# Weaving a block's message rows in pairs of slots, with both norms of the node update on ScalarE and another order of the blocks

## What is computed

```python
def _genconv(h, edge_attr, src, dst, w1, b1, g1, bb1, w2, b2, t):
    msg = relu(h[src] + edge_attr) + EPS_MSG
    m = msg * t
    seg_max = segment_max(m, dst)
    ex = exp(m - seg_max[dst])
    denom = segment_sum(ex, dst)
    alpha = ex / (denom[dst] + 1e-16)
    agg = segment_sum(msg * alpha, dst)
    out = h + agg
    z = relu(_layernorm(out @ w1 + b1, g1, bb1))      # 128 wide
    return z @ w2 + b2
h = _genconv(h0, e, ...)
for i in range(1, L):
    z = relu(_layernorm(h, ln_g[i], ln_b[i]))         # 64 wide
    h = h + _genconv(z, e, ...)
return relu(_layernorm(h, ln_g[0], ln_b[0]))
```

## Time and profile before

| | |
|---|---|
| median of 3 runs | 5808.66 us (5808.57 to 5826.21) |
| the profiled execution | 5825.41 us, its span 5823.0 us |
| TensorE, VectorE, ScalarE, GpSimd busy | 81%, 78%, 34%, 69% of the span |
| TensorE's granted clock | 0.868 of full speed |
| instructions | 108077 |

### The profile page before, as it was taken

One profiled execution on the slowest core, in us unless ns is written; L12 is line 12 of the kernel. 1 busy time (PEld: TensorE's weight loads), 2 busy tenths in 40 slices (PEclk: granted clock), 3 DMA queues, 4 the chain that ended last, 5 costly groups with the idle time before them and its releaser, 6 DMA issues.

```text
span 5823.0 us, 108077 instructions
## 1 busy us (share of the span) xinstructions
PE 4692.3 (81%) x43853; PEld 3246.1 (56%) x43853; DVE 4557.1 (78%) x8649; ACT 1992.2 (34%) x3506; POOL 4032.3 (69%) x3659
## 2 busy tenths in 40 slices
PE   6727788899958888886888798688888867896887
PEld 6726677788945554553555455355545544554544
DVE  9723555654549998996999899699989968997887
ACT  3314675665523332332233223223323322222222
POOL 2433777777637777774777777477777747777775
PEclk8966987976659999998999999899999978998988
DMA  8993777775665556554555655455565545555552
GB/s 338 413 304 111 274 282 270 263 274 211 240 218 196 183 198 181 186 200 144 181 186 200 174 192 193 148 173 198 191 174 200 184 148 177 188 189 161 177 178 96
DMA packets 317390, 1192.47 MB, mean 205 GB/s; under 512 B 139314, under 2 KB 142564, under 8 KB 249556
## 3 DMA queue, kind: packets, MB, share of 16 engines
q1 hardware_dynamic: 166676, 920.68, 42.9%
q0 software_dynamic: 128800, 209.18, 14.0%
q10 hardware_dynamic: 21408, 55.60, 2.4%
HBM read 930.35 MB, written 254.82 MB: 204 GB/s over the span
## 4 chain that ended last, share of the span: by engine, by line
DVE 35%; PE 13%; POOL 10%; issue 8%; DMA 2%; ACT 2%; SPq 0%; DVEq 0%; POOLq 0%
POOL gb L1285 9%; PE bank L1394 9%; DVE ep_layers L1384 5%; DVE xb L1318 5%; DVE ep_layers L1345 5%; DVE ep_layers L1370 4%; DVE ep_layers L1340 4%; PE bank L1302 2%; DMA gb<-ztab,ovi 2%; DVE xb L1328 1%; DVE ds L1404 1%; DVE na L1431 1%; ACT hb L282 1%; DVE st L254 1%; PE bank L1448 1%
## 5 line engine op out<-in xcount | busy, mean ns | idle before, releaser
L1285 POOL DMA_INDIRECT gb<-ztab,ovi x2512 | 2794.2, 1112 | 869.5 <-issue 736.3
L1394 PE MATMUL bank<-ep_layers,keep 128*128 128x512 f32 (+3 forms) x4928 | 2248.6, 616 | 43.2 <-DVE ep_layers L1384 43.2
L1394 PEld LDWEIGHTS bank<-ep_layers,keep 128*128 128x128 f32 x4928 | 995.9, 205 | 1241.1 <-issue 1181.8
L1302 PE MATMUL bank<-zpw,oh_layers 128*128 128x64 bf16 x28812 | 880.8, 194 | 104.2 <-DMA zpw<-ztab 104.1
L1302 PEld LDWEIGHTS bank<-zpw,oh_layers 128*128 128x128 bf16 x28812 | 874.4, 98 | 159.0 <-issue 137.1
L1131 POOL DMA_INDIRECT ecell<-zpw,ptg x588 | 627.3, 1067 | 227.8 <-issue 175.6
L1376 ACT ACTIVATE ep_layers<-ep_layers,pack 128x1280 f32<-128x1280 f32 (+14 forms) x484 | 641.9, 1347 | 190.1 <-DVE ep_layers L1370 183.9
L1370 DVE SCALAR_TENSOR_TENSOR ep_layers<-xb,bank 128x1280 f32<-128x1280 f32 (+14 forms) x484 | 689.2, 1468 | 6.8
L1384 DVE SCALAR_TENSOR_TENSOR ep_layers<-xb,ep_layers 128x1280 f32<-128x1280 f32 (+14 forms) x484 | 687.0, 1469 | 0.4
L960 PE MATMUL bank<-byk,zpw 96*102 96x102 f32 (+13 forms) x4608 | 624.3, 317 | 43.2 <-DVE zpw L941 39.4
L960 PEld LDWEIGHTS bank<-byk,zpw 96*102 96x102 f32 (+13 forms) x4608 | 609.4, 224 | 58.5 <-DVE zpw L941 49.2
(11 more groups left out here) (219 smaller groups left out, 4697.2 us busy)
## 6 DMA issues: line engine op xcount, KB each, us to landing
oh_layers<-ohd SPq DMA_DIRECT2D x196, 1568.0 KB
cb<-rowc SPq DMA_DIRECT2D x49, 1152.0 KB
ea_in<-in_ea SPq DMA_DIRECT2D x101, 512.0 KB, 9.3
enc<-es_out ACTq DMA_DIRECT2D x101, 512.0 KB
gb<-ztab,ovi POOLq DMA_INDIRECT x2512
ohd<-oh_lay SPq DMA_DIRECT2D x49, 736.0 KB
xb<-ecell SPq DMA_DIRECT2D x20, 1536.0 KB
xb<-ecell SPq DMA_DIRECT2D x20, 1504.0 KB
```

Of the source, the lines that this page charges most:

```text
L1285: at["g"][d] = ga_l[d % GB_BLOCKS](GP.indirect_dma_start(gb[:, c:c + 64], None, from_rows, bass.IndirectOffsetOnAxis(ap=ovi[:, i:i + 1], a ...
L1302: q = PE.matmul(gps[j % n_gp][:, 64 * (s % 8):64 * (s % 8) + 64], oh[:, d % 2, at_oh:at_oh + 128], zp[:, b, 64 * part:64 * part + 64], sta ...
L1394: q = PE.matmul(both[:, 0:w], ident, rows[:, 128 * (c - a):128 * (c - a) + w], start=(c == 0), stop=(c + 4 >= S.S[d]), skip_group_check=True)
```

## The change

- The sums of `add` and `over` go to a new tile `woven` instead of back to `xb`. The block's slots are cut in two halves, and slot q of the first half and slot q of the second alternate element by element: element f of the two stands at 128 q + 2 f and 128 q + 2 f + 1. So every write of `add` and `over`, and every read of `sub` and `mul`, steps 2 words. `over` becomes two instructions where the overflow slots lie in both halves, and a block with an odd number of slots gets one memset.
- `most` is one reduction over both slot indices (pairs innermost), then a maximum with 0 that writes PSUM.
- Slices are cut from the halves, up to 28 slots each. `sub` of the first three slices goes ahead of all products.
- Both norms are issued on ScalarE alone (`scalar_norm`). For the first, `first_of_pack` centres `w1` and `b1` over the 128 outputs, so that its mean is zero and only the mean square is needed.
- `node_unit` is issued in fewer and larger pieces (`run_to`), and at the end of a layer the unit before the last is finished ahead of `fold(48)`.
- The order of the blocks: V is 7, 6, 6, 5, 13, 16, 13, 15, ..., 11, 36, 11, 21, ..., 9, 16, 9, 8, 8, 8, 7. The sorted node table is written by rank and read back in five transfers by `S.runs` instead of one.

```diff
-EP_SLICES, EP_SLOTS = 3, 24
+EP_SLICES, EP_SLOTS = 3, 28
...
-        self.turn = self.ND // 2
-        ends = [d // 2 if d % 2 else self.ND - 1 - d // 2 for d in range(self.ND)]
-        self.sorted = ends[self.turn:] + ends[:self.turn]
+        few, half = self.ND - 8, (self.ND - 9) // 2
+        self.runs = [(0, 1, few + 4, 4), (4, 2, half, few - half), (5, 2, half // 2, half - half // 2),
+                     (5 + 2 * (half - half // 2), 2, 0, half // 2), (self.ND - 4, 1, few, 4)]
+        at = {p + step * i: b + i for p, step, b, n in self.runs for i in range(n)}
+        self.sorted = [at[d] for d in range(self.ND)]
...
+        def scalar_norm(A, src, width, centred, out):
+
+            total, less, square, root, half, by, fix, shift = (nwf[:, i, :] for i in range(8))
+            if not centred:
+                for s in (0, 1):
+                    q = A(AE.activation(out[:, s, 0:width], src[:, s, 0:width], ACT.Identity,
+                                        accum_out=total[:, s:s + 1]))
+                AE.wait_ge(ae_s, q)
+                q = A(AE.activation(less, total, ACT.Identity, scale=-1.0 / width))
+                AE.wait_ge(ae_s, q)
+            for s in (0, 1):
+                q = A(AE.activation(out[:, s, 0:width], src[:, s, 0:width], ACT.Square,
+                                    bias=0.0 if centred else less[:, s:s + 1],
+                                    accum_out=square[:, s:s + 1]))
+            AE.wait_ge(ae_s, q)
+            q = A(AE.activation(by, square, ACT.Ln, scale=1.0 / width, bias=eps[:, 0:1]))
+            A(AE.activation(half, square, ACT.Identity, scale=-0.5 / width, bias=eps[:, 1:2]))
+            AE.wait_ge(ae_s, q)
+            q = A(AE.activation(root, by, ACT.Exp, scale=-0.5))
...
+            for s in (0, 1):
+                q = A(AE.activation(out[:, s, 0:width], src[:, s, 0:width], ACT.Identity,
+                                    bias=0.0 if centred else shift[:, s:s + 1],
+                                    scale=root[:, s:s + 1]))
             return q
...
+            def half(t, a, b):
+                return xs[:, 128 * a:128 * b].rearrange("p (q f t) -> p t q f", t=2, f=64)[:, t]
+
+            def by_slot(t):
+                return t.rearrange("p (q f) -> p q f", f=64)
+
+            place = [(0, 0), (0, 8), (1, 0), (1, 8), (0, 16)]
...
-                x = x_of(d, lo, hi)
-                k["add"][d] = V(VE.tensor_tensor(x, gps[j % n_gp][:, 0:64 * (hi - lo)], x,
-                                                 ALU.add))
+                if j == 0 and "read" in link:
+                    vwait(link["read"])
+                t, q = place[j]
+                k["add"][d] = V(VE.tensor_tensor(
+                    half(t, q, q + hi - lo), by_slot(gps[j % n_gp][:, 0:64 * (hi - lo)]),
+                    by_slot(x_of(d, lo, hi)), ALU.add))
...
-                q = V(VE.tensor_tensor(row[:, 0:64 * m], x_of(d, 0, m), x_of(d, n - m, n), ALU.max))
+                q = V(VE.tensor_reduce(top, xs[:, 0:128 * halves(d)[0]].rearrange(
+                    "p (q f t) -> p f q t", t=2, f=64), AX.XY, ALU.max))
                 yield
-                while m > 2:
-                    vwait(q)
-                    w = m // 2
-                    q = V(VE.tensor_tensor(row[:, 0:64 * w], row[:, 0:64 * w],
-                                           row[:, 64 * (m - w):64 * m], ALU.max))
-                    m -= w
-                    if m in (6, 2):
-                        yield
                 vwait(q)
-                q = k["topx"][d] = V(VE.scalar_tensor_tensor(
-                    top, row[:, 0:64], 0.0, row[:, 64:128], ALU.max, ALU.max))
-                vwait(q)
-                q = k["topx"][d] = V(VE.tensor_copy(top_x[:, d % 2, :], top))
+                q = k["topx"][d] = V(VE.tensor_scalar(top_x[:, d % 2, :], top, 0.0,
+                                                      None, ALU.max))
...
                 k["sub"][d, i] = V(VE.scalar_tensor_tensor(
-                    ep[:, r, 0:b - a, 64:128],
-                    x_of(d, a, b).rearrange("p (s f) -> p s f", f=64), 0.0,
+                    ep[:, r, 0:b - a, 64:128], half(t, a, b), 0.0,
...
-                VE.wait_ge(pe_s, q)
-                q = yield from norm(V, A, NA[:, 0:256].rearrange("p (s c) -> p s c", s=2),
-                                    128, hb)
+                AE.wait_ge(pe_s, q)
+                q = scalar_norm(A, NA[:, 0:256].rearrange("p (s c) -> p s c", s=2), 128, True, hb)
...
-                q = yield from norm(V, A, h[:, u, :].rearrange("p (s f) -> p s f", s=2), 64,
-                                    hb)
-                yield "gap"
+                AE.wait_ge(ve_s, q)
+                q = scalar_norm(A, h[:, u, :].rearrange("p (s f) -> p s f", s=2), 64, False, hb)
+                yield "normed2"
...
                 for j in range(JS):
                     add(d, j)
                     if d + 1 < ND:
                         passes(d + 1, j)
-                    steps(2, "normed")
+                    if not ready and j == 1:
+                        run_to("turned")
+                if not ready:
+                    run_to("linear2")
...
+                if ready:
+                    run_to("rows0")
                 for _ in most(d):
...
+                    if ready:
+                        run_to("rows1")
+                for i in range(min(n, EP_SLICES)):
                     sub(d, i)
+                    if i == 0 and ready:
+                        run_to("end")
                 if d:
                     fold(d - 1)
                 if ready:
                     now.update(unit=node_unit(S.where[d - 1][0]), part=None)
-                    steps(99, "linear1")
+                    run_to("linear1")
                 for i in range(n):
                     mul(d, i)
-                    if i == n - 1:
-                        steps(4, "normed")
+                    if i + EP_SLICES < n:
+                        sub(d, i + EP_SLICES)
+                run_to("normed" if ready else "normed2")
...
-            fold(ND - 1)
-            steps(99, "end")
+            run_to("end")
             for u in k["node", "rows"]:
                 if u not in zs_at:
                     store_rows(u)
+            fold(ND - 1)
```

More of the change, by code:

```diff
@@ L1394, in mul @@
                     q = PE.matmul(both[:, 0:w], ident, rows[:, 128 * (c - a):128 * (c - a) + w],
-                                  start=(c == 0), stop=(c + 4 >= S.S[d]),
+                                  start=(i == 0 and c == a),
+                                  stop=(i == len(slices(d)) - 1 and c + 4 >= b),
                                   skip_group_check=True)
@@ L1461, in node_unit @@
                     "p (s c) -> p s c", s=2), ACT.Relu, bias=bb1, scale=g1))
+                yield "turned"
                 PE.wait_ge(ae_s, q)
@@ L1514, in node_unit @@
                     if part < 2:
-                        yield "gap"
+                        yield f"rows{part}"
                         VE.wait_ge(ae_s, q)
@@ L1530, in layer, with run_to @@
             now = {"unit": None, "part": None}
-            def steps(n, last):
-                for _ in range(n):
-                    if now["unit"] and now["part"] != last:
-                        part = next(now["unit"], "end")
-                        if part == "gap":
-                            if n < 99:
-                                return
-                            continue
-                        now["part"] = part or now["part"]
-                        if part == "end":
-                            now["unit"] = None
+            def run_to(part):
+                while now["unit"] and now["part"] != part:
+                    now["part"] = next(now["unit"], "end")
+                    if now["part"] == "end":
+                        now["unit"] = None
             def load_pack():
@@ L1591, in layer @@
                     fetch_out(d // 2)
+                ready = d and S.where[d - 1][0] != S.where[d][0]
+                n = len(slices(d))
                 for j in range(JS):
@@ L1605, in layer @@
                         gathers(e)
-                steps(2, "normed")
+                if ready:
+                    run_to("rows0")
                 for _ in most(d):
-                    steps(1, "normed")
-                ready = d and S.where[d - 1][0] != S.where[d][0]
-                n = len(slices(d))
-                if ready:
-                    sub(d, 0)
-                steps(99, "end" if ready else "turned")
-                for i in range(1 if ready else 0, n):
+                    if ready:
+                        run_to("rows1")
+                for i in range(min(n, EP_SLICES)):
                     sub(d, i)
-                steps(99, "linear2")
+                    if i == 0 and ready:
+                        run_to("end")
                 if d:
```

132 lines of the change are left out of this document (72 added, 60 removed).

## The result

The changed kernel takes 5964.77 us (median; 5947.15 to 5982.97) where before takes 5811.20 (5808.57 to 5826.21): ratio 1.0259, 95% interval 1.0223 to 1.0295. It is slower by 2.6%; 5650 had been forecast, and the range ended at 5860. The profiled execution has a span of 5980.5 us. Busy shares: TensorE 79%, VectorE 70%, ScalarE 43%, GpSimd 64%; granted clock 0.857. Only ScalarE is fuller than before (34%), which now has the norms; the other three are less full, so the time went into waits. The clock did not slow TensorE's instructions: the sums of 128x512 take 627 ns each, before 631.

The account below looks back on a forecast made before the run. GpSimd and VectorE were taken as full, TensorE at 89%. A layer's 899 us of gathers, the tail to 972 and 6 for coupling gave 978, 40 less a layer, 160 in four: 5650 us, range 5560 to 5860.

Parts of the forecast that it names:

- What bounds the kernel: Mid-layer, per 300 us: GpSimd full at 299, VectorE busy 289.16, TensorE 89%; issue of gathers soon stops VectorE's gains.
- Tree to one reduction: VectorE's maxima per block: 4.18 us replaced by one reduction of 3.44, a gain of 0.74, at worst a loss of 1.5.
- Rival C: The reduction holds GpSimd's gathers as the tree did; they stay at 958 us a layer, total 5860; chance 0.05.
- 59 us a layer from the gathers: Without the tree on VectorE, GpSimd's gathers shorten by 2.4 us a pair of blocks, 59 a layer; bounds 0 and 70.
- Norms on VectorE's side: Moving norms off VectorE saves 3.03 us a unit, 76 a layer; waiting for the second costs about 1 a unit.
- ScalarE's queue: ScalarE takes norms of 3.5 and 4.9 us a unit; behind them queue only exponentials not yet due; the first costs nothing.
- Rival B: TensorE or ScalarE sets the pace, or norms come late: 18.5 us a block, 5730 to 5780 total; chance 0.18.
- rival A: A step of 2 words costs like 4, 0.7 ns an element: 208 us more a layer, 6640 total; chance 0.17.
- Weaving: Woven adds, subtractions and products on VectorE, stepping 2 words, cost nothing extra; ends 0 and 0.7 ns an element.
- Order: With short last blocks gathers end early, engines behind them don't; GpSimd's gap between layers becomes 75 to 85 us.
- Sum: One layer: gathers 899 us, products end at 937, next first gather 972, with coupling 978; 40 less, 160 in four.
- The allowance of 6 us for three coupled engines: 6 us added to a layer's 972 because three coupled engines are near 100% busy, giving 978.

Follow-up runs that it names:

- yt_late: The changed kernel with relu(yt) and the second linear step issued behind the block's exponentials, nothing else moved: 5788.7 us, ratio 0.9951 to the kernel before.
- between_old: Changed kernel, first norm's transposes and yt between a block's slice sums, second norm ahead of next products, old block order: 5583.55 us, the fastest version.
- short_first: Changed kernel, transposes and yt between a block's slice sums, short blocks first and none in a row at the end: ratio 0.8989 to before, slow chip only.

## Why the prediction was wrong, point by point

- **What bounds the kernel: right, and too little used.** "Two engines are full and the third is at 89%" held. But the sum carried GpSimd's work, 899 us, and took its idle time from before and from one estimate at the end of a layer. Idle was the term that grew: 62.0 to 145.6.
- **Tree to one reduction: right.** 3.44 us a block, to the digit. Rival C, that the reduction holds gathers as the tree did, is out: none is long in 2617.72 to 2620.94, while the reduction runs, and those under the products and `over` are. Over the whole trace, the 307 gathers beside which VectorE did nothing but the reduction in their first 0.94 us took 985 ns at most; the 232 beside the products alone took 1628 on the average.

```profile
2617.72 3.22 DVE L1389 TENSOR_REDUCE mx<-woven 128x64 f32<-128x2944 f32 x1
2618.80 0.95 POOL L1327 DMA_INDIRECT gb<-ztab,ovi  x1 [0.30 <-issue]
2631.43 1.48 POOL L1327 DMA_INDIRECT gb<-ztab,ovi  x1 [0.30 <-issue]
2637.24 1.34 POOL L1327 DMA_INDIRECT gb<-ztab,ovi  x1 [0.30 <-issue]
```

- **59 us a layer from the gathers: right in kind, by a third too large here.** Expected about 1020 ns, measured 1048: 40 us a layer instead of 59. Measured as one part undone in the fastest version it is 55.
- **Norms on VectorE's side: right.** The second norm's wait is 137.3 / 92 = 1.5 us a unit (forecast 1). On ScalarE the first norm took 2616.65 - 2613.32 = 3.3 us (forecast 3.5), the second, 2633.85 to 2638.86, 5.0 (forecast 4.9). Worth in the fastest version: 73.1 us a layer, where 76 less the wait, some 50, had been worked out; that part was undersized.
- **ScalarE's queue: the first step that failed.** "Behind both on ScalarE queue only exponentials that aren't due yet". I looked at the norms' own length and not at what the unit issues next. yt is queued right behind the norm, its input is a transpose, and on TensorE that stands behind the sums of the block before (11.5 us on the average). Both facts were in the diff: the unit is run to its transposes and yt at the second `add`, which is ahead of the block's exponentials. That TensorE's wait for yt "is now covered by three passes" did hold, 5.2 us for 271.8; the wait had moved to ScalarE, where it was put at nothing. Cost: 49 us a layer by yt_late. Rival B named late norms at 18.5 us a block; the pair of 40.5 us is 20.2. Its price, 1000 to 1010 us a layer, doesn't follow from 18.5: by the sum used for rival A it is 49 x 18.5 + 15 + 35 = 957, and with 20.2 it is 1040.
- **Weaving: right.** A step of 2 words costs nothing, in reads and in writes; rival A (0.17) is out. The forecast had called this a guess; its reason, that two elements share a group of four words, no run tested. The reading of the Trainium skill (Vector Engine (DVE) Microarchitecture Reference, "The SBUF access granule: adjacent pairs") by which single words at a step lose the port's rate is not borne out at a step of 2: 1751 and 1756 ns for 1536 elements, against 1752 and 1751 contiguous.
- **Order: the second step that failed.** It got two sentences and no ring. "Gathers end early and the engines behind them don't" is true, and the gap at the end was seen, 75 to 85 us; it was 95.2. But it was not asked where the short blocks were taken from: the order alone costs 41.2 us a layer in the old kernel, around the block of 36 and behind it. The 44 us that GpSimd loses in the middle besides (50.4 for 6.4) belong to neither loss alone: with yt late the same order has 9.8 there, and in the old kernel 15.2. A list of V by pairs, made from the table of the kernel, would have shown without a run that blocks 24 to 27 have 79 overflow slots for 59; that a large block costs more on one position of its pair than on the other it would not have shown.
- **Sum.** Forecast for the layer from 2780.59: last gathers out at 899, products ended at 937, the next layer's first gather at 972, and 6 for coupling. Measured: 954.3, 1027.1 (3807.73), 1061.3. The tail after the products was right, 34.1 us for 35. Of the 55 that the gathers are late, 44 are the middle's idle time, and the rest comes from gathers that gave 40 us instead of 59. The products end another 35 us later than forecast after the last gather (72.8 for 38). The forecast let block 44 start as its gathers landed; VectorE came to it 29 us behind them (3686.3 and 3715.5), and from there the last five blocks took 92 us instead of 82. The allowance of 6 us for three coupled engines stood in for both failures.

The parts that were priced would have reached the 5650: without the two losses the kernel takes 5583.6.

## What to carry to other kernels

Keep a ledger of the engine that works in order and is nearly full: instructions times length, plus idle time by place. A change is priced only when both columns are, and for the idle one it is to be asked, for each wait that a queue gets, what stands behind it and what stands ahead of the instruction that ends it on its own engine. When work items of unequal size are reordered, list the sums of neighbours against the buffer that joins producer and consumer: short ones at the ends are taken from where they smoothed the flow. Such a list is a warning and no price: two orders with the same sums differed by 58 us a layer here. And where several engines are within 10% of each other, gains don't add up one at a time: here either of two parts, undone alone, returned the whole 4%.

## What the runs showed of the hardware

- VectorE reads and writes SBUF at a step of 2 words as fast as contiguously: 684 ns for 512 elements with one operand in PSUM and a woven output (684 contiguous), 1751 and 1756 ns for 1536 (1752 and 1751). The one row of a step of 4 had cost 0.7 ns an element.
- What lengthens an indirect DMA's issue on GpSimd is a VectorE operation with two SBUF operands, not the bytes that it reads. A gather takes 1139 ns on the average with the tree, 1051 with a reduction over the same slots, and 0.94 to 0.99 us under the reduction itself. The Trainium skill (SBUF — State Buffer, "Who interferes with whom") has the rule: an operation of VectorE with two SBUF inputs contends with GpSimd's reads, a reduction never does. The traces agree, and the runs add the size of the tree's part, 59.7 us a layer.
- On ScalarE an accumulating pass brings a separate read of the accumulator (0.19 us at 2613.49 and 2634.02), and a tiny operation with scale and bias from SBUF takes 379 ns, where the small ones of before were 203.
- On two of the chips TensorE's small bfloat16 products are held by "issue", for 1701.3 us in between_old on one and 1614.9 in short_first on the other, and between_old took 8058 instead of 5584 us. What it waits for there isn't in the profile.
